# A vision tower on one core: who issues the feed-forward weights and the image loads, and what the max scores read

## The chip, the cores and the metric

The kernel runs on 1 core of one Trainium2 chip. The metric is the device time of one execution in microseconds (us), lower is better. Three executions of the kernel before took 1229.97, 1231.29 and 1232.03 us; the median, 1231.29 us, is the time before.

## The reference

64 images of 3x224x224 are cut into 14x14 patches of 768 values. A linear layer makes 192 channels of each patch, two class tokens are put in front, so an image has 198 tokens. One transformer block follows: layer norm, attention with 12 heads of 16 channels and rotary embedding, a projection and a residual, then layer norm and a feed-forward block whose activations are rounded to 8 bits and whose weights are rounded to three values.

```python
h = concat([cls_tok, cls_token, patches(x) @ W_lin.T + b_lin])     # (64, 198, 192)
n = layernorm(h)
q, k, v = heads(n @ w_qkv.T)                                       # 12 heads of 16
q, k = rope(q * 16 ** -0.5), rope(k)
h = h + softmax(q @ k.T) @ v @ w_proj.T + b_proj
h = h + bitlinear(silu(gate) * up, w_out, g_out)                   # up, gate = bitlinear(layernorm(h), w_in, g_in)
```

## The kernel before

All 64 x 198 tokens lie in one row of 12672, cut into 99 tiles of 128 tokens. Five engines each run their own loop over steps s = -1 to 119, written out by hand: in each step every engine takes the next stage of several tiles or images that are in flight. TensorE embeds tile s, transposes the normalised tile s-2, projects q and k of tile s-3, transposes the rotated q and k of tile s-4, and so on; attention goes by image and by group of four heads, in half steps 2s and 2s+1. `MAX_AT`, `NMAX_AT`, `EXP_AT`, `OUT_AT` and `PROJ_AT` hold the (half) step of each such piece. All dependences are semaphores; each engine takes its instructions strictly in the written order.

The parts that the change touches:

- **q and k.** ScalarE copies the transposed q and k of a tile from PSUM to `qkd` (`copy_qkT`). SyncE's `place_qk` issues a DMA that spreads them over every other partition of `qkT`, which leaves 16 spread rows for each head. GpSimd's `round_qkT`, the first thing in its step, copies the tile from `qkT` into a second buffer `qkTr` of type fp32r. TensorE's `max_scores` multiplies from `qkTr` (31 rows for each head), DVE's `row_max` takes the negated row maxima (line L935), TensorE and ScalarE turn them round, and SyncE's `place_max` issues the small DMA `qkT<-nmaxT`, which writes them into the 32nd row of each head. `exp_scores` then multiplies 32 rows from `qkT`, and ScalarE exponentiates the result (L744).
- **The pair of GpSimd's stages behind the copy.** After `round_qkT` of tile s-4 GpSimd runs `norm_x` of tile s-1 (four instructions, L1072 to L1079), which TensorE's `transpose_xn` (L545) waits for, and `rotate` of tile s-2 (three instructions, L1091 to L1098).
- **Images.** `xp` holds three images and a margin in which the beginning of the first slot is kept again for tiles that run over the end. SyncE's `load` and `load_margin` are issued from `prepare`, behind `place_qk`, `place_v`, `place_max` and `keep_rden` of the same step. Images 1, 2 and 3 are loaded ahead of the loop.
- **Feed-forward weights.** ScalarE issues six DMAs in `load_ffn` at its step 4, some 1.5 MB in all. DVE first reads them at step 7.
- **Other transfers on SyncE's queue.** `place_v` scatters the v rows of a tile into `vaug` by image halves of 99 tokens, so a tile is cut into two or three pieces of odd row counts (97 and 31 rows for tile 82, say). `load_tab` brings a tile's bias and rotary tables.

Of the kernel before, what the change touches and what calls it, by code (L numbers as in the profile page):

```python
# [10 lines left out]
F32R = mybir.dt.float32r  # L11
# [129 lines left out]
Q_COPIES = copies(TILES, TILE, QRING)  # L141
# [14 lines left out]
def build(nc, ins, out):  # L156
# [5 lines left out]
    with ExitStack() as ctx:  # L162
# [36 lines left out]
        qkTr = sb("qkTr", [128, 2 * GROUPS, QRING], F32R)  # L199
# [87 lines left out]
        qkT_rounded = sem("qkT_rounded")  # L287
# [57 lines left out]
        def _(sp):  # L345
            def load(b):
                if b >= XSLOT:
                    sp.wait_ge(embedded, final_tile(b - XSLOT) + 1)
                at = TOKENS * (b % XSLOT)
                sp.dma_start(xp[:, :, at + TOKENS - PATCHES:at + TOKENS], x_d[b, :, :, :])\  # L350
                    .then_inc(x_loaded[b % XSLOT], 16)

            def load_margin(i):
                if MARGINS[i] > 1:
                    sp.wait_ge(embedded, MARGINS.index(MARGINS[i] - 1) + 1)
                n = beyond(i) - (TOKENS - PATCHES)
                at = XPLACES + TOKENS - PATCHES
                sp.dma_start(xp[:, :, at:at + n], x_d[final_image(i), :, :, 0:n]).then_inc(margin_loaded, 16)
# [14 lines left out]
            def prepare(i):  # L373

                if beyond(i) > TOKENS - PATCHES:
                    load_margin(i)
                if i >= FIRST_TABS:
                    load_tab(i)
                for b in range(1, IMGS - XSLOT):
                    if final_tile(b) == i - 2:  # L380
                        load(b + XSLOT)
# [61 lines left out]

            first = slice(TOKENS - PATCHES, TOKENS)
# [3 lines left out]
            load(1)  # L448
# [3 lines left out]
            load(2)  # L452
            load(XSLOT)
            for s in range(-1, STEPS):
                for b in at(OUT_AT, 2 * s + 5):
                    place_o(b)
                for b in at(NMAX_AT, 2 * s - 1):
                    place_max(b)
                for b in at(OUT_AT, 2 * s + 4):
                    place_o(b)  # L460
                for i in tile_at(s - 4):
                    place_qk(i)
                for b in at(OUT_AT, 2 * s + 3):
                    place_rec(b)
                for i in tile_at(s - 4):
                    place_v(i)
                for b in at(NMAX_AT, 2 * s):
                    place_max(b)
                for b in at(OUT_AT, 2 * s + 5):
                    keep_rden(b)  # L470
                for b in at(OUT_AT, 2 * s + 4):
                    keep_rden(b)
                for i in tile_at(s + 1):
                    prepare(i)
                for i in at(PROJ_AT, s - 7):
                    store(i)
                for b in at(OUT_AT, 2 * s + 4):
                    place_rec(b)
# [5 lines left out]
        def _(pe):  # L484
# [80 lines left out]
            def max_scores(n):  # L565
                b, g = divmod(n, GROUPS)
                pe.wait_ge(qkT_rounded, Q_COPIES[final_tile(b)])
                take_score(max_done, n + 1)
                place = TOKENS * b % QRING
                for t in range(2):  # L570
                    for r in range(4):
                        rows = slice(32 * r, 32 * r + 31)
                        last = pe.matmul(score[0:TT, r, t * TOKENS:(t + 1) * TOKENS],  # L573
                                         qkTr[rows, g, place + t * TT:place + (t + 1) * TT],
                                         qkTr[rows, GROUPS + g, place:place + TOKENS], start=True, stop=True)
                last.then_inc(maxin_ready, 1)
# [134 lines left out]
        def _(act):  # L711
            def copy_xT(i):
# [115 lines left out]
            def load_ffn():  # L828
                for t, d in ((win, win_d), (wout, wout_d)):
                    act.dma_start(t, d).then_inc(loaded_ffn, 16)  # L830
                for t, d in ((gin, gin_d), (gout, gout_d)):
                    act.dma_start(t[0:TT, :], d).then_inc(loaded_ffn, 16)
                    act.dma_start(t[TT:128, :], d[0:128 - TT, :]).then_inc(loaded_ffn, 16)

            act.wait_ge(setup_pool, SETUP_POOL)
            for s in range(-1, STEPS):
                if s == SUM_STEP - 3:
                    load_ffn()
                for n in at(EXP_AT, 2 * s - 1):
                    copy_o(n)  # L840
                for n in at(EXP_AT, 2 * s):
                    exps(n)
                for i in at(PROJ_AT, s - 4):
# [220 lines left out]
        def _(pool):  # L1064
# [37 lines left out]
            def round_qkT(i):  # L1102
                pool.wait_ge(qk_placed[i % 2], qk_count(i))
                over = (TILE * (i + 1) - 1 - QRING) // TOKENS
                if over >= 0:
                    pool.wait_ge(maxin_ready, 3 * over + 3)
                for place, _, n in pieces(TILE * i, TILE, QRING):
                    pool.tensor_copy(qkTr[:, :, place:place + n], qkT[:, :, place:place + n]).then_inc(qkT_rounded, 1)  # L1108

# [28 lines left out]
            for s in range(-1, STEPS):  # L1138
                for i in tile_at(s - 4):
                    round_qkT(i)  # L1140
# [74 lines left out]
```

## Time and profile before

| | before |
|---|---|
| median of three executions | 1231.29 us |
| the profiled execution | 1228.96 us |
| its span | 1227.2 us |
| TensorE busy (share of the span) | 1175.8 us (96%) |
| VectorE busy | 960.5 us (78%) |
| GpSimd busy | 890.6 us (73%) |
| ScalarE busy | 870.0 us (71%) |
| mean granted TensorE clock | 0.986 |
| image and margin loads on SyncE's queue | 65 and 21 issues |

The profile is of one execution. Times in its rows count from the span's start. PE is TensorE's matmuls and PEld its weight loads, DVE VectorE, ACT ScalarE, POOL GpSimd; SPq and ACTq are DMA instructions issued by SyncE and ScalarE, and their length is that of the issue, not of the transfer. A bracket behind a row gives the engine's idle time ahead of the instruction and what ended it.

### The profile page before, as it was taken

The numbers are of one execution on the slowest core, as the hardware profiler recorded it, in microseconds if no ns is written. First come the engines' busy times: TensorE is split into PE (matmuls) and PEld (weight loads), VectorE is DVE, ScalarE is ACT, GpSimd is POOL, SyncE is SP. The second block draws the span as 40 slices with busy tenths as digits, with TensorE's granted clock in tenths as the row PEclk, the third lists the DMA queues.
The fourth block names the chain that finished last, engine by engine and source line by source line (L and its number), as shares of the span: only waits on it lengthen the run. The fifth ranks groups of instructions, "written<-read, shape, count | busy, mean of one in ns | idle before, by whom it ended". The sixth has DMA issues, their size and how long they took to land.

```text
span 1227.2 us, 36712 instructions
## 1 busy us (share of the span) xinstructions
PE 1175.8 (96%) x12229; PEld 839.3 (68%) x12229; DVE 960.5 (78%) x2335; ACT 870.0 (71%) x1736; POOL 890.6 (73%) x1605
## 2 busy tenths in 40 slices
PE   6699999999999999999999999999999999999887
PEld 5566766776767767767776776776776776766556
DVE  3455787887788888888888888888888888888786
ACT  1145677777677777777777777777777787778686
POOL 3755687877677787777787777777777788776354
PEclk9889999999899999999999999999999999999899
DMA  7434433443334443444434434344343444322010
GB/s 199 138 94 112 112 95 95 130 117 94 108 96 119 118 120 91 117 127 111 124 89 120 114 99 113 91 130 108 109 122 93 117 122 114 90 80 71 28 50 29
DMA packets 201611, 129.17 MB, mean 105 GB/s; under 512 B 55114, under 2 KB 200725, under 8 KB 201333
## 3 DMA queue, kind: packets, MB, share of 16 engines
q1 hardware_dynamic: 198852, 123.70, 37.2%
q10 hardware_dynamic: 2576, 3.14, 1.0%
q8 instruction: 102, 1.67, 0.6%
q14 instruction: 81, 0.66, 0.2%
HBM read 66.57 MB, written 10.70 MB: 63 GB/s over the span
## 4 chain that ended last, share of the span: by engine, by line
PE 80%; DMA 6%; DVE 5%; ACT 3%; issue 2%; SPq 2%; POOL 2%; ACTq 0%; POOLq 0%; DVEq 0%
PE turn L535 15%; PE score L593 12%; PE turn L615 10%; PE turn L553 10%; PE turn L644 6%; PE score L573 5%; PE turn L602 5%; DMA qkT<-nmaxT 4%; PE turn L623 3%; DVE nmax L935 3%; PE turn L561 2%; PE turn L662 2%; PE turn L624 2%; PE turn L517 2%; PE turn L545 2%
## 5 line engine op out<-in xcount | busy, mean ns | idle before, releaser
L935 DVE TENSOR_REDUCE nmax<-score 99x8 f32<-99x1584 f32 x192 | 347.3, 1809 | 165.3 <-PE score L573 165.3
L744 ACT ACTIVATE prob<-score 99x1584 f32<-99x1584 f32 x192 | 286.4, 1492 | 95.4 <-PE score L593 95.1
L535 PE MATMUL turn<-wlin,xp 128*128 128x192 f32 x1188 | 228.0, 344 | 8.0 <-DMA xp<-in_x 8.0
L535 PEld LDWEIGHTS turn<-wlin,xp 128*128 128x128 f32 x1188 | 198.9, 197 | 18.1 <-issue 8.8
L593 PE MATMUL score<-qkT 32*99 32x198 f32 x3072 | 179.2, 347 | 12.8 <-DVE nmax L935 7.7
L615 PE MATMUL turn<-prob,vaug 99*32 99x198 f32 x3072 | 168.3, 338 | 0.0
L1122 POOL TENSOR_TENSOR yg<-early,gout 128x512 f32<-128x512 f32 x99 | 125.8, 1271 | 46.9 <-ACT yr L808 41.5
L593 PEld LDWEIGHTS score<-qkT 32*99 32x99 f32 x3072 | 116.1, 161 | 56.0 <-issue 39.3
L553 PE MATMUL turn<-wqkv,xT 96*128 96x384 f32 x396 | 151.7, 506 | 0.0
L767 ACT ACTIVATE xiT<-turn 96x256 bf16<-96x256 bf16 x99 | 37.5, 379 | 128.6 <-PE turn L633 128.4
L615 PEld LDWEIGHTS turn<-prob,vaug 99*32 99x32 f32 x3072 | 80.9, 109 | 63.7 <-issue 37.1
L1091 POOL TENSOR_TENSOR ropec<-qk,tab 128x384 f32<-128x384 f32 x99 | 99.0, 1000 | 17.5 <-ACT qk L724 17.3
L775 ACT ACTIVATE early<-turn,fxh 128x512 f32<-128x512 f32 x99 | 68.1, 688 | 55.7 <-PE turn L644 55.3
L1098 POOL TENSOR_TENSOR qkp<-ropec,ropes 128x384 f32<-128x384 f32 x99 | 100.2, 1013 | 7.8
L644 PE MATMUL turn<-winq,xiT 96*128 96x512 bf16 x396 | 103.5, 384 | 1.7 <-ACT xiT L767 1.4
L1093 POOL TENSOR_TENSOR ropes<-qk,tab 128x384 f32<-128x384 f32 x99 | 99.0, 1000 | 0.0
L1108 POOL CAST qkTr<-qkT 128x768 fp32r<-128x768 f32 (+15 forms) x114 | 85.9, 760 | 16.4 <-DMA qkT<-qkd 16.3
L553 PEld LDWEIGHTS turn<-wqkv,xT 96*128 96x128 f32 x396 | 67.8, 190 | 42.5 <-issue 15.8
L573 PE MATMUL score<-qkTr 31*99 31x198 f32 x1536 | 83.6, 291 | 9.1 <-ACT prob L744 7.0
L1113 POOL TENSOR_SCALAR ve<-mv 128x1 f32<-128x1 f32 x99 | 18.8, 190 | 97.1 <-DVE mv L928 96.0
L602 PE MATMUL turn<-wqkv,xT 96*128 96x192 f32 x396 | 85.3, 338 | 0.0
L573 PEld LDWEIGHTS score<-qkTr 31*99 31x99 f32 x1536 | 50.6, 160 | 43.9 <-issue 38.8
(94 smaller groups left out, 2406.1 us busy)
## 6 DMA issues: line engine op xcount, KB each, us to landing
xp<-in_x SPq DMA_DIRECT2D x63, 588.0 KB, 5.1
qkT<-qkd SPq DMA_DIRECT2D x84, 192.0 KB, 2.5
tab<-joined SPq DMA_DIRECT2D x98, 112.0 KB, 2.7
orec<-rden_kept SPq DMA_DIRECT2D x192, 49.5 KB
out<-h SPq DMA_DIRECT2D x99, 96.0 KB, 3.0
onum<-osb SPq DMA_DIRECT2D x64, 99.0 KB, 2.6
vaug<-vt SPq DMA_DIRECT2D x30, 148.5 KB
onum<-osb SPq DMA_DIRECT2D x64, 49.5 KB, 2.3
```

Of the source, the lines that this page charges most:

```text
L535: last = pe.matmul(turn[:, k, 0:D], xp[:, c, place:place + TILE], wlin[:, c, :], start=(c == 0), stop=(c == KC - 1))
L553: last = pe.matmul(turn[:, k, 0:QK], xT[:, i % 2, c, :], wqkv[:, c, 0:QK], start=(c == 0), stop=(c == 1))
L573: last = pe.matmul(score[0:TT, r, t * TOKENS:(t + 1) * TOKENS], qkTr[rows, g, place + t * TT:place + (t + 1) * TT], qkTr[rows, GROUPS + g, ...
L593: last = pe.matmul(score[0:TT, r, t * TOKENS:(t + 1) * TOKENS], qkT[rows, GROUPS + g, place + t * TT:place + (t + 1) * TT], qkT[rows, g, p ...
L602: last = pe.matmul(turn[:, k, 0:D], xT[:, i % 2, c, :], wqkv[:, c, QK:3 * D], start=(c == 0), stop=(c == 1))
L615: last = pe.matmul(turn[32 * r:32 * r + 32, k, 0:TOKENS], vaug[:, b % VRING, t, VHEAD * hd:VHEAD * hd + VHEAD], prob[:, t, hd, :], start=( ...
L644: last = pe.matmul(turn[:, k + half, :], xiT[:, i % TBUF, c, :], winq[:, c, half * FF:(half + 1) * FF], start=(c == 0), stop=(c == 1))
L744: act.activation(prob[:, :, 4 * g:4 * g + 4, :].rearrange("p t r n -> p r t n"), score[0:TT, :, 0:2 * TOKENS].rearrange("p r (t n) -> p r ...
L935: dve.tensor_reduce(nmax[:, b % 2, :, g:HEADS:GROUPS].rearrange("p t r -> p r t"), score[0:TT, :, 0:2 * TOKENS].rearrange("p r (t n) -> p ...
L1091: pool.tensor_tensor(ropec[:, :].rearrange("p (h e f) -> p h e f", e=DH // 2, f=2), src, cos, ALU.mult)\
L1098: pool.tensor_tensor(qkp[:, i % 2, :].rearrange("p (c d h) -> p h c d", c=GROUPS, h=2), *(r[:, :].rearrange("p (h c d) -> p h c d", c=GROU ...
L1122: pool.tensor_tensor(yg[:, i % 2, :], y[:, i % 2, :], gout[:, :], ALU.mult).then_inc(yg_ready, 1)
```

## The change

Three edits:

1. The buffer `qkTr`, the semaphore `qkT_rounded` and GpSimd's `round_qkT` go. `qkTr` becomes a view of `qkT` as fp32r, and `max_scores` waits for the placing DMAs of the image's last two tiles itself.
2. SyncE issues the feed-forward weights, once, in its step 3, right behind tile 4's tables; ScalarE no longer does at its step 4.
3. The loads of images 3 to 63 and of the margins move from SyncE's `prepare` to a new `bring` on ScalarE, which stands behind `exps` of half step 2s in each step, with the same waits. Images 0, 1 and 2 stay on SyncE ahead of the loop. `prepare` keeps the tables.

```diff
-        qkTr = sb("qkTr", [128, 2 * GROUPS, QRING], F32R)
+        qkTr = qkT[:, :, :].bitcast(F32R)
@@ SyncE
             def prepare(i):
-                if beyond(i) > TOKENS - PATCHES:
-                    load_margin(i)
                 if i >= FIRST_TABS:
                     load_tab(i)
-                for b in range(1, IMGS - XSLOT):
-                    if final_tile(b) == i - 2:
-                        load(b + XSLOT)
...
+            def load_ffn():
+                for t, d in ((win, win_d), (wout, wout_d)):
+                    sp.dma_start(t, d).then_inc(loaded_ffn, 16)
+                for t, d in ((gin, gin_d), (gout, gout_d)):
+                    sp.dma_start(t[0:TT, :], d).then_inc(loaded_ffn, 16)
+                    sp.dma_start(t[TT:128, :], d[0:128 - TT, :]).then_inc(loaded_ffn, 16)
...
-            load(2)
-            load(XSLOT)
+            load_first(2)
...
                 for i in tile_at(s + 1):
                     prepare(i)
+                if s == SUM_STEP - 4:
+                    load_ffn()
@@ TensorE
             def max_scores(n):
                 b, g = divmod(n, GROUPS)
-                pe.wait_ge(qkT_rounded, Q_COPIES[final_tile(b)])
+                for i in range(max(final_tile(b) - 1, 0), final_tile(b) + 1):
+                    pe.wait_ge(qk_placed[i % 2], qk_count(i))
                 take_score(max_done, n + 1)
@@ ScalarE
+            def load(b):
+                act.wait_ge(embedded, final_tile(b - XSLOT) + 1)
+                at = TOKENS * (b % XSLOT)
+                act.dma_start(xp[:, :, at + TOKENS - PATCHES:at + TOKENS], x_d[b, :, :, :])\
+                    .then_inc(x_loaded[b % XSLOT], 16)
...
+            def bring(i):
+
+                if beyond(i) > TOKENS - PATCHES:
+                    load_margin(i)
+                for b in range(IMGS - XSLOT):
+                    if final_tile(b) == i - 2:
+                        load(b + XSLOT)
...
             for s in range(-1, STEPS):
-                if s == SUM_STEP - 3:
-                    load_ffn()
                 for n in at(EXP_AT, 2 * s - 1):
                     copy_o(n)
                 for n in at(EXP_AT, 2 * s):
                     exps(n)
+                for i in tile_at(s + 1):
+                    bring(i)
@@ GpSimd
-            def round_qkT(i):
-                pool.wait_ge(qk_placed[i % 2], qk_count(i))
-                over = (TILE * (i + 1) - 1 - QRING) // TOKENS
-                if over >= 0:
-                    pool.wait_ge(maxin_ready, 3 * over + 3)
-                for place, _, n in pieces(TILE * i, TILE, QRING):
-                    pool.tensor_copy(qkTr[:, :, place:place + n], qkT[:, :, place:place + n]).then_inc(qkT_rounded, 1)
...
             for s in range(-1, STEPS):
-                for i in tile_at(s - 4):
-                    round_qkT(i)
```

## Rows read from the trace of the kernel before

**Rows 1.** The page's busy times of the whole span, by engine.

```profile
PE 1175.8 (96%) x12229; PEld 839.3 (68%) x12229; DVE 960.5 (78%) x2335; ACT 870.0 (71%) x1736; POOL 890.6 (73%) x1605
```

**Rows 2.** Stretches: length, busy (and count) by engine, PEclk, DMA share, GB/s.

```profile
30.00:60.00 30.00, 18.89 (x109) 14.55 (x109) 13.85 (x21) 4.88 (x13) 22.43 (x32) 0.89 0.51 144
320.00:1100.00 780.00, 776.30 (x8320) 549.99 (x8313) 650.18 (x1593) 596.18 (x1196) 608.45 (x1102) 1.00 0.41 110
```

**Rows 3.** The page's costliest groups: busy, mean ns, idle before, releaser.

```profile
L1108 POOL CAST qkTr<-qkT 128x768 fp32r<-128x768 f32 (+15 forms) x114 | 85.9, 760 | 16.4 <-DMA qkT<-qkd 16.3
L573 PE MATMUL score<-qkTr 31*99 31x198 f32 x1536 | 83.6, 291 | 9.1 <-ACT prob L744 7.0
L573 PEld LDWEIGHTS score<-qkTr 31*99 31x99 f32 x1536 | 50.6, 160 | 43.9 <-issue 38.8
```

**Rows 4.** Timeline, 24 to 30 us: start, length, engine, line, operation, [idle, releaser].

```profile
24.04 0.32 ACTq L830 DMA_DIRECT2D early<-in_win  x1
24.09 0.48 ACT L730 ACTIVATE qkd<-turn 128x384 f32<-128x384 f32 x1
...
24.67 0.65 SPq L401 DMA_DIRECT2D qkT<-qkd  x1
...
25.12 0.42 PE L545 MATMUL turn<-ident,xn 128*96 128x128 f32 x2 [0.47 <-POOL xn L1079]
...
26.62 0.38 ACT L717 ACTIVATE xT<-turn 96x256 f32<-96x256 f32 x1 [2.05 <-issue]
...
27.06 1.00 POOL L1098 TENSOR_TENSOR qkp<-ropec,ropes 128x384 f32<-128x384 f32 x1
...
28.98 0.81 PE L602 MATMUL turn<-wqkv,xT 96*128 96x192 f32 x4
...
29.75 3.52 SPq L401 DMA_DIRECT2D qkT<-qkd  x1
```

**Rows 5.** Timeline, 32 to 43 us.

```profile
32.99 0.82 POOL L1108 CAST qkTr<-qkT 128x768 fp32r<-128x768 f32 x1 [4.93 <-DMA qkT<-qkd]
...
35.19 0.50 POOL L1079 TENSOR_SCALAR xn<-h,nm,rstd 128x192 f32<-128x192 f32 x1
...
35.75 0.66 PE L545 MATMUL turn<-ident,xn 128*96 128x128 f32 x2 [5.95 <-POOL xn L1079]
...
42.39 0.43 PE L573 MATMUL score<-qkTr 31*99 31x198 f32 x8 [0.23 <-POOL qkTr L1108]
```

**Rows 6.** Stretches of the start, columns as in rows 2.

```profile
20.00:24.00 4.00, 4.00 (x25) 3.38 (x24) 0.90 (x3) 0.99 (x4) 3.52 (x6) 1.00 0.09 20
...
30.00:36.00 6.00, 0.25 (x2) 0.25 (x3) 0.00 (x0) 0.00 (x0) 2.66 (x6) 0.82 0.96 255
```

**Rows 7.** SyncE's image loads (line L350): issue in ns, min/median/max.

```profile
L350 SPq DMA_DIRECT2D xp<-in_x x63: 546/622/1715, 4.3 to 1054.6; - x63
```

**Rows 8.** Timeline near the end of the tiles, TensorE.

```profile
1128.21 0.43 PE L573 MATMUL score<-qkTr 31*99 31x198 f32 x8 [1.11 <-POOL qkTr L1108]
```

**Rows 9.** Timeline, 950 to 954 us, ScalarE and SyncE's queue.

```profile
950.44 1.49 ACT L744 ACTIVATE prob<-score 99x1584 f32<-99x1584 f32 x1 [0.44 <-PE score L593]
...
951.24 1.69 SPq L390 DMA_DIRECT2D vaug<-vt  x2
953.50 1.41 SPq L435 DMA_DIRECT2D qkT<-nmaxT  x1
```

**Rows 10.** The stretch behind that issue, columns as in rows 2.

```profile
953.00:957.00 4.00, 4.00 (x40) 3.33 (x39) 3.90 (x13) 2.46 (x7) 2.68 (x5) 1.00 0.08 27
```

**Rows 11.** Timeline, TensorE's exp scores (L593): one tile's run at full clock.

```profile
962.22 0.93 PE L593 MATMUL score<-qkT 32*99 32x198 f32 x16 [1.11 <-DMA qkT<-nmaxT]
...
968.02 0.93 PE L593 MATMUL score<-qkT 32*99 32x198 f32 x16
```

**Rows 12.** The same run of instructions in a spell of half clock.

```profile
305.42 0.93 PE L593 MATMUL score<-qkT 32*99 32x198 f32 x16 [2.08 <-DMA qkT<-nmaxT]
...
314.41 0.93 PE L593 MATMUL score<-qkT 32*99 32x198 f32 x16
```

More of the change, by code:

```diff
@@ L138, in copies @@
     return np.cumsum([len(pieces(size * n, size, ring)) for n in range(stretches)]).tolist()
-Q_COPIES = copies(TILES, TILE, QRING)
 O_COPIES = copies(IMGS, TOKENS, ORING)
@@ L286, in build @@
         qk_placed = [sem(f"qk_placed{p}") for p in range(2)]
-        qkT_rounded = sem("qkT_rounded")
         maxin_ready = sem("maxin_ready")
@@ L345, in _, with load_first @@
         def _(sp):
[L346 to L358, printed above, removed]
+            def load_first(b):
+                at = TOKENS * b
+                sp.dma_start(xp[:, :, at + TOKENS - PATCHES:at + TOKENS], x_d[b, :, :, :]).then_inc(x_loaded[b], 16)
             def load_tab(i):
@@ L447, in _ @@
             load_tab_parts(0)
-            load(1)
+            load_first(1)
             sp.wait_ge(tables_joined, 16 * 6)
@@ L711, in _, with load_margin @@
         def _(act):
+            def load(b):
[3 more added lines that the diff above has]
+                    .then_inc(x_loaded[b % XSLOT], 16)
+            def load_margin(i):
+                if MARGINS[i] > 1:
+                    act.wait_ge(embedded, MARGINS.index(MARGINS[i] - 1) + 1)
+                n = beyond(i) - (TOKENS - PATCHES)
+                at = XPLACES + TOKENS - PATCHES
+                act.dma_start(xp[:, :, at:at + n], x_d[final_image(i), :, :, 0:n]).then_inc(margin_loaded, 16)
+            def bring(i):
[4 more added lines that the diff above has]
+                        load(b + XSLOT)
             def copy_xT(i):
@@ L827, in _ @@
                 act.dma_start(t[...], d).then_inc(loaded_attn, 16)
[L828 to L833, printed above, removed]
             act.wait_ge(setup_pool, SETUP_POOL)
             for s in range(-1, STEPS):
-                if s == SUM_STEP - 3:
-                    load_ffn()
                 for n in at(EXP_AT, 2 * s - 1):
```

## The prediction, made before the changed kernel ran

> **What bounds the kernel now.** I read the busy times first [rows 1]: TensorE is busy 96% of the span, no other engine above 78%. The table by stretches then says where that holds [rows 2]: from 320 to 1100 us TensorE is busy 776.3 of 780 us at full clock, so nothing that only relieves GpSimd, ScalarE or SyncE can shorten that part; but from 30 to 60 us it is busy only 18.9 of 30 us and its mean clock is 0.89. So the gain has to come from the start, from the few idle spots later, and from the clock. The timeline of the start shows the largest idle time of the whole trace [rows 4, 5]: TensorE finishes `project_v` of step 4 at 29.8 us (28.98 + 0.81) and starts its next matmul at 35.75, after 5.95 us of waiting for `xn`. `xn` was late because GpSimd stood at its copy until 32.99, 4.93 us idle, waiting for the DMA that placed tile 0's q and k. That DMA was issued at 24.67, 0.6 us behind the first feed-forward weight [rows 4]. The DMA engines then ran at 0.96 of their time up to 36 us, while from 20 to 24 us they had run at 0.09 [rows 6].
>
> **Edit 1, no copies.** It removes 114 copies, 85.9 us of GpSimd [rows 3]. In the steady part GpSimd has slack and TensorE has none, so that is worth nothing there. In the start it takes the DMA wait out of GpSimd's queue, where `norm_x` and `rotate` stood behind it. I work out when the first `max_scores` runs, 42.39 us now [rows 5]. GpSimd ends `rotate` of tile 1 at 28.06 (27.06 + 1.00) [rows 4]. `norm_x` takes 1.88 us, from the end of the copy, 33.81, to 35.69 [rows 5], so `xn` is ready at 29.9, and `rotate`, three passes of about 1.00 us, ends near 32.9. TensorE can start L545 at 30.0. From that L545 to the end of the following transposes took 3.86 us at full clock in the step before (25.12 to 28.98) [rows 4], so `max_scores` comes at about 33.9, and `rotate`'s 32.9 is in time for its transposes. That is 8.5 us earlier; 5.9 us of it are idle time, the rest is the half-speed clock that followed the idle time (clock 0.82 in the mean of 30 to 36 us [rows 6]).
> From there to 60 us DVE holds the chain (row maxima, sums of the weights), and its work does not change, so I carry the 8.5 us on unchanged and add nothing.
> Near the end there is one more wait for the copy, 1.11 us at 1128.21 [rows 8]; it goes. The next release there is a score buffer, and I count 1.1 us, with 0 as the lower bound if the exponentials take over.
> The edit adds one wait on TensorE for each of 192 `max_scores`, less for image 0. Queued behind it is everything on TensorE. The semaphores will have been set long before, so the price is that of a passed wait. Its bounds: zero, as TensorE's idle time ahead of L573 has no share from issue (9.1 us, of which 7.0 for ScalarE and the rest for the copy), and half of the issue time in front of the weight loads, 38.8 / 2 = 19 us, since there are two waits now [rows 3]. It can't be below nothing, as it only adds an instruction. I take zero, because the matmul row is the one in which the engine's time is counted and the weight loads run beside it.
>
> **Edit 2, weights by SyncE in step 3.** Nothing in SyncE's steps up to 3 waits for data of the loop, so they are issued at about 16 us, behind the second image, instead of 24.04 us on ScalarE. 1.5 MB at the 255 GB/s of rows 6 are 6 us, and the quiet stretch from 20 to 24 us takes most of them. Queued behind them in SyncE's queue is `place_qk` of tile 0, which can't be issued before 24.67 anyway, and of tile 1, at 29.75. That one is needed at 33.9; the issue alone took 3.52 us when the queues were full [rows 4], and should take about the 0.65 us of the row at 24.67. On ScalarE the six issues go that delayed `copy_xT` at 26.62 (2.05 us idle, put down to issue) [rows 4]; TensorE was still embedding then, so this is worth nothing by itself. The edits overlap: either alone would remove most of the 5.95 us, so I count the 8.5 us once.
>
> **Edit 3, images by ScalarE.** 61 images and 21 margins are issued by ScalarE. One issue takes 0.62 us in the median and up to 1.72 [rows 7]. The weights' issue at 24.04 ran beside the copy of 24.09 to 24.57, which stands ahead of it in the program [rows 4], so ScalarE's queue issues while an ACTIVATE still runs, and `bring` stands behind an exponential of 1.49 us [rows 9]: I take zero in the steady part. The cover is gone in steps without an exponential, that is in the first eight; there it is 0 to 0.6 us once, at the table load, and I take 0.3. If the cover failed throughout, 82 x 0.62 = 51 us would fall on ScalarE, idle 29% of the span.
> The images no longer stand behind the step's placements, but with 3.7 us of idle time in 780 [rows 2] TensorE has no wait for images to lose, so nothing is gained. What they collide with is the other side. The latest `qkT<-nmaxT` of the steady part land 8.7 us and more after the issue: issued 953.50, waited for until 962.22 [rows 9, 11]. Meanwhile the DMA engines worked at a share of 0.08, little more than one of sixteen [rows 10]: `place_v`, issued at 951.24 with pieces of 97 and 31 rows, is crawling through one engine and the maxima wait behind it. By the pieces of the tiles this is so in three steps (29 and 77 with 67 and 61 rows, 86 with 97 and 31), and nearly in three more (18, 43, 63). Before, SyncE issued the image of step 86 after the maxima. Now ScalarE issues it during the exponential of 950.44, just ahead of `place_v` [rows 9]. An image takes about 5 us to land, of which one sixteenth of the work, 588 KB / 16 at the 255/16 GB/s of rows 6, is 2.3 us on that one engine. So the maxima come later by 0 to 2.3 us; I take 1, for steps 18 and 86, which have both: 2 us. Each can also bring a spell of half clock. Its price: the same run from L593 to L593 took 8.99 us at half clock (305.42 to 314.41) and 5.80 at full (962.22 to 968.02), 3.2 us [rows 11, 12].
> The Trainium skill bears on this. Its page "DMA: Bandwidth & Descriptors", section "Why a DMA increments its semaphore by 16 and not by 1", says that a copy runs on the largest number of engines up to 16 that divides its row counts, so that 97 and 31 rows use one each. By that rule the trace agrees: 128 rows at 1536 B on one engine explain the share of 0.08. The same page, section "Issuing engines are not separate DMA queues", says that another issuing engine saves only issue time, as all go through the same 16 engines. By that rule the third edit can't speed up any landing and gives 0 us of gain where a private lane for the images would give something; it is the reason why my rival C below is not dismissed.
>
> **The sum.** Against the profiled execution, 1228.96 us (span 1227.2 and 1.8 around it): -8.5 - 1.1 + 0.3 + 2.0 = -7.3 us, 1221.7 us. The profiled execution is 2.3 us faster than the median of three. Against the median 1231.3 that is 1224.0.
>
> **Rivals.**
> A (forecast, 0.55): as worked out, 1224; its own range is 1221 to 1227, from 0 or 2.3 us for each of the collisions and 0 or 1.1 us at the end.
> B (0.20): the shift by 8.5 us also frees other spells of half clock. The mean clock of 0.986 means 2 x 0.014 x 1227 = 34 us at half clock in all, of which the start's spell is a part and the one at 306 [rows 12] another; each that goes gives 3.2 us, so one or two of them 1221 to 1217.5. For it: the one at 306 followed 2.08 us of idle time, while the 1.11 us of 962.22 were followed by none [rows 11, 12], so it takes little to tip it. Against: that wait, for the maxima of step 29, remains.
> C (0.06), slower: images and margins in ScalarE's queue delay the maxima behind `place_v` in the four late steps that have one (18, 63, 77, 86), each by 2.3 us of idle time and a spell of 3.2 us, 22 us in all, less the 9.3 gained: 1244. It decides against the change when two of them happen in full (11 us). Against: in two of the four it is a margin, which is small, and the image is issued before `place_v`, so part of it is done by then.
> D (0.12): the first `max_scores` is still late since the weights now stand ahead of the placements in the same queue; if tile 1's placement lands 4 us later than needed, at 38, half of the gain is left: 1228.
> E (0.07): the added wait shows on TensorE with 0.05 us, a quarter of the issue time in front of a weight load [rows 3]: 192 x 0.05 = 9.6 us, no change: 1233 at most.
>
> **How the numbers follow.** The likeliest case gives 1224.0. From the low end of B's second spell to D's end, 1217 to 1229, 8 in 10 is held. About 0.2% (2.5 us) can be told from no change, so 1228.8 and 1233.8 are the borders: A and B are faster, D for the larger part, E is the same, C slower, with a little of E: faster 0.85, same 0.09, slower 0.06.
>
> **What would show it.** The first L573 at about 34 us instead of 42.4 and no idle time over 1 us ahead of L545 at 30 us; image issues on ScalarE's queue inside the L744 rows with no new idle time "issue" on ScalarE; no wait at the last tiles; the maxima of steps 18 and 86 later by about 1 us. The prediction is wrong if TensorE's busy time outside the start grows, if L573 gains idle time before it, or if spells of half clock appear at steps where there were none.

## The result and the profile after

The changed kernel takes 1241.53 us (median of ten executions, 1233.01 to 1248.34). The kernel before takes 1232.16 us in the same series (1228.56 to 1239.78). The ratio is 1.0068, with a 95% interval from 1.0044 to 1.0093: slower by some 8 us, where 7 us of gain were forecast. One and the same kernel varies by 10 to 15 us from execution to execution, so versions are compared by medians and intervals, and single profiles only show where something happens.

| | before | after |
|---|---|---|
| the profiled execution | 1228.96 us | 1239.81 us |
| its span | 1227.2 us | 1238.0 us |
| TensorE busy / idle in the span | 1175.8 / 51.4 us | 1181.8 / 56.2 us |
| GpSimd busy | 890.6 us | 808.1 us |
| mean granted TensorE clock | 0.986 | 0.979 |

The page's busy times of the kernel after, for [rows 1], and the steady stretch of [rows 2] and those of [rows 6] again, with 24 to 30 us beside them (length, busy and count of PE, PEld, DVE, ACT and POOL, PEclk, DMA share, GB/s):

```profile
PE 1181.8 (95%) x12229; PEld 845.4 (68%) x12229; DVE 950.8 (77%) x2335; ACT 870.5 (70%) x1736; POOL 808.1 (65%) x1491
...
320.00:1100.00 780.00, 774.30 (x8257) 548.09 (x8250) 635.96 (x1582) 592.64 (x1187) 547.56 (x1013) 1.00 0.41 109
...
20.00:24.00 4.00, 4.00 (x23) 3.48 (x22) 0.80 (x3) 1.11 (x3) 2.43 (x3) 1.00 0.95 212
24.00:30.00 6.00, 2.40 (x13) 1.40 (x11) 0.64 (x3) 1.48 (x4) 5.40 (x10) 0.88 1.07 276
30.00:36.00 6.00, 3.88 (x13) 3.85 (x14) 0.06 (x1) 0.00 (x0) 1.07 (x2) 0.55 0.20 60
```

GpSimd lost 82 us of work and TensorE gained nothing from it. The weights did move into the quiet stretch: the DMA engines work at 0.95 from 20 to 24 us, 0.09 before. Yet TensorE is busy only 2.40 us from 24 to 30, and has a clock of 0.55 in the six after it. The timeline of that place (PE, and the issues of both queues), and behind them one row of the chain of waits:

```profile
16.54 0.61 ACTq L707 DMA_DIRECT2D xp<-in_x  x1
20.93 0.56 ACTq L715 DMA_DIRECT2D xp<-in_x  x1
32.12 3.79 PE L526 MATMUL turn<-wlin,xp 128*128 128x192 f32 x12 [5.24 <-DMA xp<-in_x]
42.66 0.44 PE L565 MATMUL score<-qkT 31*99 31x198 f32 x8 [0.69 <-DMA qkT<-qkd]
...
20.93 10.94 DMA xp<-in_x
```

The wait for `xn` of [rows 5] is gone, and one of 5.24 us has taken its place: tile 4 can't be embedded. Its margin, a small load, was issued by ScalarE at 20.93, behind image 3 (16.54) and beside the weights in SyncE's queue, and landed 10.94 us later. The first `max_scores` runs at 42.66 us, as in [rows 5] (42.39).

The costliest groups that answer to [rows 3], and the two that changed most (busy, mean ns, idle ahead and what ended it); behind them a row of DVE's waits (total, times, longest):

```profile
L565 PE MATMUL score<-qkT 31*99 31x198 f32 x1536 | 83.9, 291 | 11.2 <-ACT prob L757 8.9 <-DMA qkT<-qkd 2.1
L565 PEld LDWEIGHTS score<-qkT 31*99 31x99 f32 x1536 | 50.9, 161 | 46.1 <-issue 43.0 <-DMA qkT<-qkd 3.1
L526 PE MATMUL turn<-wlin,xp 128*128 128x192 f32 x1188 | 231.7, 348 | 13.8 <-DMA xp<-in_x 13.8
L585 PE MATMUL score<-qkT 32*99 32x198 f32 x3072 | 180.2, 349 | 16.7 <-DVE nmax L941 9.4 <-DMA qkT<-nmaxT 7.3
...
DVE onT L958 <- DMA orec<-rden_kept: 12.1, 9, 2.8
```

TensorE's wait for images grew from 8.0 to 13.8 us, the one for the maxima (`qkT<-nmaxT`) from 5.0 to 7.3 us, and DVE now waits nine times for the denominators of the softmax (`orec<-rden_kept`), which it never did before. All three are DMAs. One wait for the denominators reaches TensorE:

```profile
101.94 1.25 DVE L958 TENSOR_TENSOR onT<-onum,orec 128x396 f32<-128x396 f32 x1 [2.75 <-DMA orec<-rden_kept]
...
105.05 0.93 PE L585 MATMUL score<-qkT 32*99 32x198 f32 x16 [1.74 <-DVE nmax L941]
```

DVE takes its row maxima behind the instruction that waited, and TensorE waits for those: the step of 1.2 us between n = 8 and n = 15 in the next table.

Where the 10.8 us of span come from shows in the start times of single `max_scores`. TensorE runs them in a fixed order, so the n-th can be set beside the n-th. Difference to the kernel before in us, profiled executions; the columns are explained with the experiments:

```
n     before   after   e12    e15    e5    e10    e14    e13
0       42.4    +0.3   -5.9   -6.1   -4.0   -4.0   -5.6   -7.0
8       84.8    +1.1   -4.6   -4.9   -2.7   -1.7   -4.8   -6.9
15     121.1    +2.3   -4.6   -4.9   -1.5   -1.4   +1.2   -7.0
30     209.6    +3.5   -5.1   -4.0   -0.2   -1.1   +0.7   -7.4
50     328.6    +5.0   -6.1   -1.3   -2.9   -5.3   -4.0  -12.8
150    917.7    +5.4   -6.0   -1.1   +2.0   -2.1   -4.3  -14.8
160    976.4   +10.6   -6.0   +4.6   +7.0   -1.7   -5.5  -16.0
191   1159.1    +8.5   -9.9   +2.2  +10.1   -4.7   -6.9  -13.0
```

Single profiles also differ by where a spell of half clock falls (e14's 6 us between n = 8 and 15 is one, clock 0.50 from 100 to 108 us), so sizes are taken from the medians. The profiled execution of e12 is 5.5 us below e12's own median, so its column flatters it.

Against e12, the kernel without the third edit, the kernel after is 6.2 us late at n = 0, another 5 us by n = 50, and then loses most between n = 150 and 160: 5.2 us, at step 86, one of the two steps for which the forecast had counted 1 us each.

```profile
955.83 1.49 ACT L757 ACTIVATE prob<-score 99x1584 f32<-99x1584 f32 x1 [0.44 <-PE score L585]
955.83 0.56 ACTq L707 DMA_DIRECT2D xp<-in_x  x1
956.61 3.52 SPq L373 DMA_DIRECT2D vaug<-vt  x2
958.56 0.30 ACT L750 ACTIVATE nmaxT<-turn 12x198 f32<-12x198 f32 x1
960.17 1.71 SPq L418 DMA_DIRECT2D qkT<-nmaxT  x1
969.63 0.93 PE L585 MATMUL score<-qkT 32*99 32x198 f32 x16 [3.14 <-DMA qkT<-nmaxT]
978.62 0.93 PE L585 MATMUL score<-qkT 32*99 32x198 f32 x16
...
958.00:960.00 2.00, 2.00 (x16) 1.97 (x13) 1.90 (x2) 1.38 (x5) 1.27 (x1) 1.00 0.97 296
```

Read it against [rows 9, 11]. The image is issued 0.8 us ahead of the v pieces. While it moves (share 0.97, 296 GB/s), issuing the two v pieces takes SyncE 3.52 us instead of 1.69. So the maxima, ready at 958.86, are issued only at 960.17, 1.3 us late, and that issue takes 1.71 us. TensorE gets them 9.46 us after that, 8.72 before. Counted from the issue of the v pieces it is 13.02 us (956.61 to 969.63) instead of 10.98 (951.24 to 962.22). TensorE waits 3.14 us instead of 1.11: 2.0 us more. Before, the clock stayed up and the next run of L593 came after 5.80 us [rows 11]; now it comes after 8.99 us (969.63 to 978.62), at half clock, the very price of [rows 12]: 3.2 us more. 2.0 + 3.2 = 5.2 us. At step 18, the other of the two, the same wait is 1.00 us (at 181.82) instead of 0.24 (at 178.74), close to the 1 us of the forecast, and the clock stays up.

### The profile page after: what moved, and what is told of

Read it like the earlier page. It is cut to its first block, busy times and chain, and to the rows that moved or that the text cites. A ratio compares the mean times of both kernels' runs of the same rounds, so it can differ in the third digit from the quotient of the medians.

```text
span 1238.0 us, 36506 instructions
## 1 busy us (share of the span) xinstructions
PE 1181.8 (95%) x12229; PEld 845.4 (68%) x12229; DVE 950.8 (77%) x2335; ACT 870.5 (70%) x1736; POOL 808.1 (65%) x1491
## 3 DMA queue, kind: packets, MB, share of 16 engines
q8 instruction: 102, 1.67, 0.6%
## 4 chain that ended last, share of the span: by engine, by line
PE 83%; DMA 7%; DVE 4%; ACT 2%; issue 2%; SPq 2%; POOL 0%; ACTq 0%; DVEq 0%; POOLq 0%
PE turn L526 16%; PE score L585 13%; PE turn L607 10%; PE turn L544 10%; PE turn L636 6%; PE score L565 5%; PE turn L594 5%; PE turn L615 4%; DMA qkT<-nmaxT 3%; DVE nmax L941 2%; PE turn L552 2%; PE turn L654 2%; PE turn L616 2%; PE turn L508 2%; PE turn L536 2%
## 5 line engine op out<-in xcount | busy, mean ns | idle before, releaser
L526 PE MATMUL turn<-wlin,xp 128*128 128x192 f32 x1188 | 231.7, 348 | 13.8 <-DMA xp<-in_x 13.8
L526 PEld LDWEIGHTS turn<-wlin,xp 128*128 128x128 f32 x1188 | 202.8, 200 | 24.0 <-issue 14.8
L1128 POOL TENSOR_SCALAR vsq<-ss,kap 128x1 f32<-128x1 f32 x99 | 34.0, 344 | 132.1 <-ACT junk L795 132.1
L565 PE MATMUL score<-qkT 31*99 31x198 f32 x1536 | 83.9, 291 | 11.2 <-ACT prob L757 8.9
L565 PEld LDWEIGHTS score<-qkT 31*99 31x99 f32 x1536 | 50.9, 161 | 46.1 <-issue 43.0
```

What stands on the lines that cost most here:

```text
L526: last = pe.matmul(turn[:, k, 0:D], xp[:, c, place:place + TILE], wlin[:, c, :], start=(c == 0), stop=(c == KC - 1))
```

## The experiments

All ratios are against the kernel before in the same series on the same chip, with 95% intervals; differences in us are (ratio - 1) x 1231. "Edit 3" is the images and margins on ScalarE. In the code cuts "..." stands for lines left out.

### One part at a time

**e1, edit 1 alone.**

```diff
-        qkTr = sb("qkTr", [128, 2 * GROUPS, QRING], F32R)
+        qkTr = qkT[:, :, :].bitcast(F32R)
...
```

> The kernel before with edit 1 alone (no copies, max scores on the spread rows). Theory M, that the third edit (images and margins in ScalarE's queue) is what costs time: this run is no slower than before; GpSimd no longer waits, but the first max scores still need tile 1's placement, which landed at 41.4 us before, so at most 1 to 3 us are gained, ratio 0.997 to 1.000. Theory N, that the lost copies or the added waits on TensorE cost time in the steady part: slower by 5 to 10 us, ratio 1.004 to 1.008, with TensorE idle time put down to issue or to the placements.

Measured: 1230.35 us, 0.9982 [0.9956, 1.0009], no change that can be told.

```profile
30.74 3.04 SPq L399 DMA_DIRECT2D qkT<-qkd  x1
33.83 4.32 SPq L388 DMA_DIRECT2D vaug<-vt  x2
43.03 0.66 PE L572 MATMUL score<-qkT 31*99 31x198 f32 x8 [8.05 <-DMA qkT<-qkd]
```

GpSimd no longer stands, but with the weights still in the way tile 1's placement lands late, and TensorE waits 8.05 us for that instead of 5.95 for `xn`. So the copy only passed the wait on.

**e2, edit 2 alone.**

```diff
+                if s == SUM_STEP - 4:
+                    load_ffn()        # on SyncE; gone on ScalarE
...
```

> The kernel before with edit 2 alone (feed-forward weights issued by SyncE in step 3). Theories M and N both: tile 0's placement lands at about 27 us instead of 32.9, the idle time ahead of tile 3's transpose goes, first max scores at 35 us instead of 42.4, 7 us faster, ratio 0.994.

Measured: 1225.16 us, 0.9939 [0.9915, 0.9963]. The first `max_scores` runs at 39.2 us.

**e12, edits 1 and 2**, images as before.

> Edits 1 and 2 without edit 3 (the changed kernel with images and margins back in SyncE's queue). Theory M: the 8.5 us of the prediction appear, first max scores near 34 us, 1223 us, ratio 0.992 to 0.994. Theory N: slower than before or the same, ratio 0.999 to 1.005.

Measured: 1224.75 us, 0.9935 [0.9906, 0.9964]: 8.0 us faster than before.

Rows of SyncE's queue and of TensorE, at the start and at step 86, and between them one row of the chain of waits:

```profile
29.93 0.66 SPq L399 DMA_DIRECT2D qkT<-qkd  x1
36.48 0.66 PE L581 MATMUL score<-qkT 31*99 31x198 f32 x8 [2.32 <-DMA qkT<-qkd]
...
29.93 6.41 DMA qkT<-qkd
...
945.01 1.67 SPq L388 DMA_DIRECT2D vaug<-vt  x2
947.54 1.17 SPq L433 DMA_DIRECT2D qkT<-nmaxT  x1
956.25 0.93 PE L601 MATMUL score<-qkT 32*99 32x198 f32 x16 [1.12 <-DMA qkT<-nmaxT]
```

No margin is late, tile 1's placement takes 0.66 us to issue as forecast, and the first `max_scores` runs at 36.5 us, 5.9 earlier; at step 86 all is as in [rows 9, 11]. So these two edits together do what the forecast said, nearly in size, and edit 2 alone carries the gain: e2 and e12 can't be told apart.

**e3, edit 3 alone.**

```diff
                 for n in at(EXP_AT, 2 * s):
                     exps(n)
+                for i in tile_at(s + 1):
+                    bring(i)          # margin and image, on ScalarE
...
```

> The kernel before with edit 3 alone (images 3 on and all margins issued by ScalarE). Theory M: slower by 5 to 10 us or more, ratio 1.004 to 1.010, with a wait for xp ahead of the embedding of tile 4 in the start, and 2 us more idle time at step 86 with a spell of half clock behind it. Theory N: same as before, ratio 0.998 to 1.002.

Measured: 1241.41 us, 1.008 [1.0049, 1.0111]. Edit 3 is the whole loss: 9.8 us by itself. The expected wait for tile 4's margin isn't there, though ScalarE issues it at 20.94 as in the kernel after; the weights are issued only from 25.38 on here. The late margin takes edits 2 and 3 together. Its trace has waits of 11.0 us for the denominators and 6.7 us for the maxima.

### The start

**e5, the changed kernel with image 3 and the margin of tile 4 given back to SyncE**, ahead of the weights.

```diff
             load_first(2)
+            sp.wait_ge(embedded, final_tile(0) + 1)
+            sp.dma_start(xp[:, :, TOKENS - PATCHES:TOKENS], x_d[XSLOT, :, :, :]).then_inc(x_loaded[0], 16)
+            ...                       # and the margin of tile 4
```

> The changed kernel with image 3 and tile 4's margin issued by SyncE ahead of its loop, as before; images 4 on and the other margins stay with ScalarE. If the loss in the start is the margin's late issue behind image 3 in ScalarE's queue: no wait for xp ahead of tile 4's embedding, first max scores at about 36 us, 6 us faster than the changed kernel, 1235 us, ratio 1.002; what is left above the 1225 us of edits 1 and 2 is the third edit's cost in the steady part. If the start's loss has another cause (the weights' bytes as such): ratio stays at 1.007.

Measured: 1239.28 us, 1.0072 [1.0045, 1.0099].

```profile
38.43 0.66 PE L569 MATMUL score<-qkT 31*99 31x198 f32 x8 [3.41 <-DMA qkT<-qkd]
...
PE score L589 <- DMA qkT<-nmaxT: 7.7, 4, 2.9
```

The wait for the margin is gone and the first `max_scores` comes 4 us earlier than before, but the median doesn't follow. In its profile the lead shrinks to 0.2 us by n = 30 and is a loss of 10.1 us at n = 191. The late margin is why the changed kernel lost its gain at the start, and not why it is slower.

### Place in time, queue, bytes

**e7, e5 with `bring` half a step later on ScalarE**, just ahead of `exps` of half step 2s+1.

```diff
-                for i in tile_at(s + 1):
-                    bring(i)
...
+                for i in tile_at(s + 1):
+                    bring(i)
                 for n in at(EXP_AT, 2 * s + 1):
                     exps(n)
```

> As e5_start_sp, with ScalarE's image and margin issues moved some 5 us later in its step, in front of the exponentials of half step 2s+1, so that an image no longer goes out just ahead of place_v and the maxima. Theory R, that the images' bytes share the DMA engines with SyncE's small transfers: the waits for the maxima fall back to about 5 us and the time by 3 to 8 us against e5_start_sp, ratio 0.996 to 0.999, unless they now meet the denominators instead. Theory I, that the issue as such delays ScalarE: no change against e5_start_sp or worse, ratio 1.002 to 1.005.

Measured: 1244.23 us, 1.0114 [1.0075, 1.0153]. The waits for the denominators fall to 2.8 us, those for the maxima grow to 13.2 us (9 times, up to 3.7), and the kernel is as slow or slower. Neither theory had this: the waits for the maxima were expected to fall. Step 86 shows why they don't.

```profile
960.24 1.89 SPq L418 DMA_DIRECT2D qkT<-nmaxT  x1
962.21 0.55 ACTq L711 DMA_DIRECT2D xp<-in_x  x1
971.49 1.66 PE L589 MATMUL score<-qkT 32*99 32x198 f32 x16 [3.70 <-DMA qkT<-nmaxT]
```

Here the image is issued 2.0 us behind the maxima, and they are late all the same: TensorE waits 3.70 us for them. Counted from the issue of the v pieces (at 958.53, in 1.65 us) it is 12.96 us, where e12 has 11.24 (945.01 to 956.25) with an image 4.5 us behind the maxima in their own queue. The waits for the maxima as a whole are 9 against e12's 5. So an image in the other queue seems to slow even what was issued before it.

**e15, e12 with the images issued by SyncE ahead of the v pieces**: nearly the changed kernel's place in time, but one queue.

```diff
+                if s >= 4:
+                    for i in tile_at(s + 1):
+                        images(i)     # margin and image, no longer in prepare
                 for i in tile_at(s - 4):
                     place_v(i)
```

> Edits 1 and 2 alone, and from step 4 on SyncE issues the image and the margin of its step between the placement of q and k and the placement of v, not at the end of its step. So the images are in flight at the same time as in the changed kernel, but in one queue with the maxima. Theory S (sharing between two queues costs: in one queue only what was issued before is ahead, and the maxima lose no more than the image's part on their engines, at most 2.3 us at each of four steps, with a half-clock spell at one or two of them): 1226 to 1232 us, waits of TensorE for qkT<-nmaxT 8 to 14 us. Theory P (position alone: whatever puts the image ahead of the v pieces costs, whichever queue it is in): 1236 to 1242 us as with edit 3, with waits for the denominators of 10 us.

Measured: 1233.0 us, 0.9983 [0.9951, 1.0016].

```profile
949.85 0.63 SPq L348 DMA_DIRECT2D xp<-in_x  x1
950.57 3.59 SPq L390 DMA_DIRECT2D vaug<-vt  x2
952.09 0.30 ACT L752 ACTIVATE nmaxT<-turn 12x198 f32<-12x198 f32 x1
954.21 1.74 SPq L435 DMA_DIRECT2D qkT<-nmaxT  x1
963.59 0.93 PE L608 MATMUL score<-qkT 32*99 32x198 f32 x16 [3.57 <-DMA qkT<-nmaxT]
...
PE score L608 <- DMA qkT<-nmaxT: 10.2, 5, 3.6
```

At step 86 this is the changed kernel's picture with one queue: v pieces 3.59 us in the issue, maxima issued 1.8 us late, 5.7 us lost between n = 150 and 160. Counted from the issue of the v pieces TensorE gets the maxima after 13.02 us (950.57 to 963.59), as in the kernel after. So what costs at this step is that an image stands ahead of the v pieces, whoever issues it. Against e12 the medians say 5.9 us for the whole kernel (the intervals overlap).

e5, with two queues, is another 11 us slower, and those intervals are apart. The time and the waits for the maxima are those of Theory S; e15 has no wait for denominators, where Theory P had 10 us and e5 has 12.4. That isn't the queue alone, though. e15 issues each image behind the step's placement of q and k and behind the denominators. ScalarE in e5 doesn't keep that order, as a later pair of steps shows, e5 first:

```profile
637.45 0.55 ACTq L719 DMA_DIRECT2D xp<-in_x  x1
637.48 1.49 SPq L384 DMA_DIRECT2D qkT<-qkd  x2
639.07 1.72 SPq L413 DMA_DIRECT2D orec<-rden_kept  x3
...
638.36 1.35 SPq L401 DMA_DIRECT2D qkT<-qkd  x2
639.81 1.73 SPq L430 DMA_DIRECT2D orec<-rden_kept  x3
642.22 0.65 SPq L348 DMA_DIRECT2D xp<-in_x  x1
```

From 60 to 1040 us, 29 of e5's 73 image and margin issues stand less than 2.5 us ahead of a placement of q and k and 14 so far ahead of denominators; none of e15's do. (e12 has 14 and 19 such cases, in one queue, and is fast, so place alone need not be it.) The page's median landing of the placements is 2.8 us in e5 and 2.5 in e15. So place and queue differ between the two at once, and how the 11 us divide is not shown. By the table e5 is behind e15 by 2.2 us at n = 8 and by 3.8 at n = 30, ahead by 1.6 at n = 50, and behind by 3.1 at n = 150 and 7.9 at n = 191: no single place.

**e9, e12 and 61 issues by ScalarE besides, one for each image that edit 3 moves, with 8 bytes in each packet**, into memory that nobody reads. The images themselves stay on SyncE; the margins have no such issue.

```diff
+            def small(i):
+                for b in range(IMGS - XSLOT):
+                    if final_tile(b) == i - 2:
+                        act.wait_ge(embedded, final_tile(b) + 1)
+                        act.dma_start(scrap[:, b, :, :], x_d[b + XSLOT, :, :, 0:2]).then_inc(scrapped, 16)
```

> Edits 1 and 2, images by SyncE, and ScalarE issues in the place of each image a DMA of as many packets with 8 bytes in each into an unused tile: the issue and the packets without the bytes. Theory R: as edits 1 and 2 alone, 1225 us, ratio 0.993 to 0.995. Theory I: 5 to 8 us slower than those, ratio 0.998 to 1.001.

Measured: 1227.79 us, 0.9972 [0.9945, 0.9999]. By the medians 4.6 us more than e12, with overlapping intervals: the issues and packets without the bytes are at most the smaller part.

**e11, e5 with half of each image from number 4 on.** It leaves out half of the embedding's input.

```diff
-                act.dma_start(xp[:, :, at + TOKENS - PATCHES:at + TOKENS], x_d[b, :, :, :])\
+                act.dma_start(xp[:, 0:KC // 2, at + TOKENS - PATCHES:at + TOKENS], x_d[b, :, 0:KC // 2, :])\
```

> e5_start_sp with only the first three of six 128-row chunks of images 4 on loaded, so half of ScalarE's image bytes and packets; the embedding of these images uses stale values in the other half. Theory R (the bytes cost): about half of the 14 us between edits 1 and 2 and e5_start_sp comes back, 1232 us, ratio 1.000 to 1.002; the wait at step 86 is shorter by about 1 us. Theory I (the issues cost): the same as e5_start_sp, ratio 1.007.

Measured: 1231.53 us, 0.9986 [0.9958, 1.0014]: e5 is 16.9 us above e12, and 10.6 us of that go with half the bytes and packets. Waits for denominators: 4.8 us. With e9 this says that the loss is mostly the moving of bytes.

### The maxima and the v pieces

**e8, e12 with the maxima issued ahead of the v pieces; e10, the same in e5.**

```diff
+                for b in at(NMAX_AT, 2 * s):
+                    place_max(b)
                 for i in tile_at(s - 4):
                     place_v(i)
-                for b in at(NMAX_AT, 2 * s):
-                    place_max(b)
```

> Edits 1 and 2, images by SyncE, and SyncE places the maxima of half step 2s ahead of the v rows instead of behind them. If the late maxima come from the one-engine pieces of v ahead of them in the same queue: no wait of the exp scores for the maxima is left (5.6 us of idle time in edits 1 and 2) and the spell of half clock behind step 29 goes, 5 to 8 us faster than edits 1 and 2, ratio 0.987 to 0.990. If SyncE's waiting for the maxima holds up the v rows instead: waits ahead of the weighed values (L615) and no gain.

> e5_start_sp (images 4 on by ScalarE, start as before) with SyncE placing the maxima of half step 2s ahead of the v rows. Theory R1, that the third edit costs by making the maxima behind the one-engine v pieces later: the waits for the maxima at steps 18, 29, 77 and 86 (7.7 us in e5_start_sp) and the half-clock spells behind them go, and with them most of the loss: 1225 to 1229 us, ratio 0.996 to 0.999. Theory R2, that it costs mainly through the denominators (12.4 us of DVE idle for them) or something else: no more than 5 us gained, ratio 1.003 or above.

Measured: e8 1222.87 us, 0.9943 [0.9916, 0.997]; e10 1227.17 us, 0.9967 [0.9941, 0.9993].

```profile
951.37 0.59 SPq L418 DMA_DIRECT2D qkT<-nmaxT  x1
952.06 1.34 SPq L373 DMA_DIRECT2D vaug<-vt  x2
...
L589 PE MATMUL score<-qkT 32*99 32x198 f32 x3072 | 179.2, 347 | 10.5 <-DVE nmax L945 10.5
...
DVE onT L962 <- DMA orec<-rden_kept: 25.7, 20, 3.1
```

e10 is the changed kernel with two small repairs. The order of two issues gives 12.9 us against e5 (intervals apart), where without ScalarE's images it gives nothing that can be told (e8 against e12). The 5 to 8 us that were expected of e8 did not come, though its wait for the maxima is gone: its trace has two new waits for images in their place, 1.1 us at 425 and 1.8 at 851, the second with half clock behind it. e10 has no wait for maxima, and 25.7 us for the denominators, twice those of e5: most of DVE's waits for `orec` are a sign of the same crowding, and not what sets the time.

**e13, e12 with each v piece cut into a part of a multiple of 16 rows and the rest; e14, the same in e5; e16, e13 with the maxima first.**

```diff
+        m = 16 * (n // 16)
+        out += [(p + lo, half, at + lo, size) for lo, size in ((0, m), (m, n - m)) if size]
...
-                for p, half, at, n in token_runs(i):
+                for p, half, at, n in v_runs(i):
```

> Edits 1 and 2, images by SyncE, and each v piece issued as a DMA of a multiple of 16 rows and one of the rest (97 rows as 96 and 1). If a piece of an odd row count crawls through one DMA engine: no stretch with a DMA share of 0.08 behind steps 29, 77 and 86, no wait for the maxima, 5 us faster than edits 1 and 2, ratio 0.987 to 0.991. If the added issues (some 220 of 0.6 us) bind SyncE: waits for placements, ratio 0.996 or above.

> e5_start_sp with the v pieces split in the same way. Theory R1 (image bytes in a second queue hurt what waits behind the one-engine pieces): the third edit's cost is gone with them, the time within 3 us of e13_split, ratio 0.988 to 0.993. If the third edit costs without the one-engine pieces too: 5 us or more above e13_split.

> Edits 1 and 2 alone, the v pieces split into a part with a multiple of 16 rows and the rest, and the maxima issued ahead of the v pieces. If the maxima's wait behind the v pieces was all that the split removed, the second measure adds nothing: 1215 to 1218 us, as with the split alone, with no wait for qkT<-nmaxT in either. If the split still leaves the maxima behind one-engine rests, 2 us less: 1213 to 1215.

Measured: e13 1216.35 us, 0.9877 [0.9846, 0.9907]; e14 1218.76 us, 0.9904 [0.9868, 0.9939]; e16 1217.08 us, 0.986 [0.981, 0.991].

```profile
936.27 2.80 SPq L397 DMA_DIRECT2D vaug<-vt  x4
938.41 0.30 ACT L754 ACTIVATE nmaxT<-turn 12x198 f32<-12x198 f32 x1
939.12 0.60 SPq L442 DMA_DIRECT2D qkT<-nmaxT  x1
...
L610 PE MATMUL score<-qkT 32*99 32x198 f32 x3072 | 179.8, 348 | 7.7 <-DVE nmax L943 7.7
```

In e13 the four v pieces of step 86 take 2.80 us to issue where two took 1.67, yet all waits for the maxima are gone, and it gains 7.1 us on e12 (the intervals just touch). By the table 5.4 us of it come between n = 30 and 50, where e12 waits 2.70 us for the maxima of step 29. It beats the kernel before by 15 us and is the best version here. In e14 the same cut takes 20.7 us from e5, so that images on ScalarE cost only 3.3 us more than on SyncE (overlapping intervals) instead of 16.9. The maxima first add nothing to that (e16 against e13). The Trainium skill gives a rule for the cut, in "DMA: Bandwidth & Descriptors", section "Why a DMA increments its semaphore by 16 and not by 1": the row count's largest divisor up to 16 is the number of engines, so that 97 rows go through one and 96 through sixteen. By that rule e13's result is what one expects; the trace agrees in that the maxima no longer wait, and no row shows single engines. Every piece whose row count isn't a multiple of 16 is cut, so the gain isn't that of one pair of row counts.

## Why the prediction was wrong

**Right.** The bound, and where the gain had to come from. Edit 2's working: the weights fill the quiet stretch, and the gain of edits 1 and 2 together was -9.6 us in the sum and -8.0 us in e12 (interval -11.6 to -4.4). The added wait on TensorE costs nothing that shows: L565 has no idle time from issue ahead of its matmuls, and e12 isn't slower than e2. Rival E is out with that. B's extra spell of half clock at 306 stayed, in e12 and in the kernel after.

**The size at the start.** The first `max_scores` was put at 33.9 us and came at 36.5 in e12. What was missing is of rival D's kind: tile 1's placement is issued in time (29.93), but takes 6.41 us to land, where the page's median for such placements is 2.5 us. The v pieces of tile 0 (25.54) and an image (27.73) stand ahead of it in the same queue. The sum had the issue of that transfer and no time for its landing.

**"Either alone would remove most of the 5.95 us"** was wrong for edit 1: in e1 a wait for the placement took its place. I had followed the chain to the copy and not asked when the next user of the same DMA would be released.

**The step that failed: edit 3 gains nothing and costs 2.0 us plus 0.3.** It measured 9.8 us alone and about 16 us on top of edits 1 and 2 (e12 to the changed kernel, 0.9935 to 1.0068). Three things in it were wrong.
- *Which issues move, and behind what.* In the trace of before SyncE issues the margin of tile 4 at 15.88 us. The prediction counted the 21 margins as issues and never asked when this one would land. ScalarE issued it at 20.93, it landed at 31.87, and the 5.24 us of waiting and the spell behind it used up all that edits 1 and 2 gave at the start. With edit 3 alone the same margin makes nobody wait (e3), so it was its meeting with edit 2's weights that was missed.
- *The collision at step 86.* The place was right and the mechanism was rival C's. The size was not: 1 us was taken, and 2.0 us of wait plus 3.2 us of half clock came. The 2.0 us are within the forecast's own bounds (0 to 2.3 us, one sixteenth of an image on the one engine), at their upper end. The spell is what is missing: written down as a price, it was left out of the sum, though 1.11 us of wait stood already there [rows 11] and 2.08 us elsewhere had been followed by one [rows 12]. That the issue of the v pieces doubles (1.69 to 3.52 us) was not foreseen either; in e7 it doesn't (1.65 us) and the maxima are late all the same, so it isn't shown to be the cause.
- *The other small transfers.* The denominators and the placements are slowed by the image too: DVE's 12.1 us for the denominators, of which one wait cost TensorE 1.74 us. They were not in the sum, as TensorE and DVE had no wait for them in the trace of before.

Rival C gave 1244 at 0.06, and that the measured 1241.5 lies beside it is luck. Of its four steps one came in full (86, 5.2 us of 5.5); step 18 took 0.8 us more, steps 63 and 77 nothing. The rest came from tile 4's margin, from small waits and from spells elsewhere. Its argument against, that the image is issued before the v pieces and so partly done, didn't help: with 0.8 us of lead 2.0 of the 2.3 us came.

**The end.** -1.1 us for the copy's wait at 1128 [rows 8] came to nothing; the lower bound held. At the same instruction the changed kernel waits as long, for the exponentials:

```profile
1138.83 0.43 PE L565 MATMUL score<-qkT 31*99 31x198 f32 x8 [1.11 <-ACT prob L757]
```

**Still open.** What the second queue costs by itself. e5 against e15 has 11 us for queue and place together. The runs show that the loss goes with the image's bytes (e11), that it passes through the maxima and the v pieces (e10, e14), and that the maxima can be late with the image issued behind them (e7), but not how the engines are shared out. No run issues the images at exactly the same moments from either queue. How much is pure clock is open as well: over the ten executions of the changed kernel the time falls by about 1.06 us for each 0.001 of mean clock, and TensorE's busy time is 6.0 us of its 10.8 us of longer span.

## What to carry to other kernels

Before a bulk load is moved to an idle engine's queue, list the small latency-bound transfers in flight in the same stretch, above all behind copies whose row counts are odd: here they paid for it in the landing and in the clock. Cost every DMA of the moved step, the small ones first. And when a wait moves from one engine to another, ask when the *DMA* behind it lands, since removing what only passes the wait on brings nothing (e1: 5.95 us became 8.05).

## What the hardware showed that was not expected

- Issuing the two v pieces of step 86 (97 and 31 rows) takes 1.65 to 1.69 us with no image just ahead (before, e12, e7) and 3.12 to 3.59 us with one issued 0.5 to 0.8 us before, from the same queue or the other (after, e3, e5, e15). An image alone doesn't do it: in e15 three pieces 0.7 us behind an image (at 628.61) take 2.48 us, in e12 without one 2.54.
- Cutting each v piece into a multiple of 16 rows and the rest (97 into 96 and 1), in a copy for which no trace has a wait, gave 7 us (e13) and 21 us (e14) of some 1230.
- The second queue is no private lane. In e7 an image issued there 2.0 us behind the maxima goes with their landing 1.7 us later than in e12, counted from the v pieces. The Trainium skill's "DMA: Bandwidth & Descriptors", section "Issuing engines are not separate DMA queues", says that another issuing engine only saves issue time. The traces agree at step 86, where the maxima take 13.02 us from the v pieces with either queue (after, e15). For the whole kernel e5 is 11 us slower than e15, but as its images are also issued at other places, no run here shows that the rule fails.
